# Local attention: the query projection of a tile moved ahead of the output projection and the scores on TensorE

## The chip, the core and the metric

The kernel runs on one core of a Trainium2 chip. The time is the device time of the launch in microseconds (us), as the median of the runs; the profile is one execution of the same program. Five queues work side by side and meet only at semaphores: TensorE (PE; its weight loads are listed as PEld), VectorE (DVE), ScalarE (ACT), GpSimd (POOL) and SyncE (SP), which issues transfers.

## The reference, cut to what matters

Four blocks stand in a row: cross attention, a feed-forward block that is a two-layer local transformer, cross attention again, and a mixture of experts. The change touches the local attention inside the second block, which runs once for each of its two layers (16 sequences of 256 tokens, 8 heads of 64, windows of 64 tokens):

```python
def _layer(x, wqkv, qs, ksc, wo, ...):
    h = shift_token(x)
    q, k, v = jnp.split(h @ wqkv, 3, axis=-1)     # then split into heads
    q = l2norm(q) * qs
    k = l2norm(k) * ksc
    q, k = rotary_xpos(q, k)
    o = local_attention(q, k, v)                  # own and previous window
    x = x + o @ wo
    ...                                           # feed-forward part
```

The order in which the tiles' projections are computed has no effect on the values.

## The kernel before

The 16 x 256 tokens are 32 tiles of 128 tokens (T = 32). Class Local holds local attention as a software pipeline: in step s each engine works on several tiles of different age, and its program is written out by hand, step after step. Nothing is scheduled by a tool; every engine runs its own list in order and waits where a semaphore tells it to. Local runs for l = 0 and l = 1, one tile in each step.

In a step s, TensorE's list (method tensor) is:

- the values of tile s-4 into the bank ps_b (project_h, three 128x512 matmuls at L947 to L949);
- the output projection of tile s-7 into ps_a (L990);
- the masks and scores of tile s-4 into ps_s (L1004 and L963);
- the queries of tile s-1 into the first half of ps_qk (project_h again);
- the transposes of rotated queries and keys of tile s-3 (L1032) and of the input of tile s (L1043);
- attention weights times values of tile s-6 (L1057), the transposes of the weights of tile s-5 (L1068);
- the keys of tile s-1 into the second half of ps_qk.

VectorE's list in the same step (method vector) is: reciprocal of the softmax sums of tile s-5 (L1174), addition of the output projection of tile s-7 to the residual (L1178, "the y addition" below), the sums of squares of tile s-2 (L1184), the row maxima of the scores of tile s-4 (L1191) and their scaling (L1195), the copy of transposed queries of tile s-3 (L1202), the two products of the keys' rotation of tile s-2 (L1156, L1158), the copy of the attention output of tile s-6 (L1215), the low part of the transposed input of tile s (L1221), and last the two products of the queries' rotation of tile s-1 (L1156, L1158 again).

ps_qk has one copy. So the query projection of tile s-1 may overwrite its first half only when ScalarE has squared the queries of tile s-2 out of it and VectorE has rotated them, which is the last thing on VectorE's list in step s-1. Two lines of the projection say so, with k the number of the tile counted over both layers:

```python
after(pe, self.s_sq, 2 * (k - 1) + 1)
after(pe, self.s_r, 4 * (k - 1) + 2)
```

GpSimd adds the two products of a rotation (L1260 for queries, L1272 for keys), multiplies the exponentials by the reciprocal (L1266) and scales the keys (L1279). ScalarE squares queries and keys (L1103, L1142), takes the eight exponentials of a tile (L1135) and copies transposed results. The neighbouring stages overlap the first and the last steps of Local.

Of the kernel before, what the change touches and what calls it, by code (L numbers as in the profile page):

```python
# [19 lines left out]
T = B * S // P  # L20
# [6 lines left out]
INNER = LH * LD  # L27
# [74 lines left out]
def after(eng, sem, count):  # L102

    if count > 0:
        eng.wait_ge(sem, count)
# [775 lines left out]
class Local(Phase):  # L881
# [83 lines left out]
    def tensor(self, pe, l, s):  # L965
        g = self.g
        ps_qk, ps_t, ps_a, ps_b, ps_s = self.banks[l]
# [6 lines left out]
        n = s - 4  # L974
        if 0 <= n < T:
            k = T * l + n
            after(pe, self.s_vc, k)
            after(pe, self.s_oc, k - 2)
            if n == 0:
                self.take(pe, l, "b")  # L980
            self.project_h(pe, ps_b[:, :], n, 1024).then_inc(self.s_v, 1)
        n = s - 7
        if 0 <= n < T:
            k = T * l + n
# [8 lines left out]
        n = s - 4  # L993
        if 0 <= n < T:
            k, u, b = T * l + n, n % 2, n // 2
# [12 lines left out]
                    for x in range(2):  # L1008
                        m = self.scores(pe, ps_s, pair, e, x, u, b)
            m.then_inc(self.s_s, 1)  # L1010
        n = s - 1
        if 0 <= n < T:
            k = T * l + n
            pe.wait_ge(self.s_hc, k + 1)
            pe.wait_ge(self.s_hr, k + 1)
            after(pe, self.s_sq, 2 * (k - 1) + 1)
            after(pe, self.s_r, 4 * (k - 1) + 2)
            if n == 0:
                self.take(pe, l, "qk")
            self.project_h(pe, ps_qk[:, 0:INNER], n, 0).then_inc(self.s_qk, 1)  # L1020
        n = s - 3
        if 0 <= n < T:
            k = T * l + n
# [10 lines left out]
        n = s  # L1034
        if 0 <= n < T:
            k = T * l + n
# [7 lines left out]
        n = s - 6  # L1044
        if 0 <= n < T:
            k, u, b = T * l + n, n % 2, n // 2
# [14 lines left out]
        n = s - 5  # L1061
        if 0 <= n < T:
            k = T * l + n
# [6 lines left out]
        n = s - 1  # L1070
        if 0 <= n < T:
            k = T * l + n
# [750 lines left out]
```

## Time and profile before

| | |
|---|---|
| median of 3 runs | 1166.66 us (1161.32 to 1167.23) |
| the profiled execution's own time | 1164.99 us |
| its span, first to last instruction | 1162.5 us |
| PE busy | 1074.8 us (92%) |
| DVE busy | 967.7 us (83%) |
| ACT busy | 932.1 us (80%) |
| POOL busy | 762.9 us (66%) |

Local attention occupies about 165 to 420 us and 500 to 770 us of the span. In the steady part of either layer a step takes 7.62 us. Busy shares say little by themselves here: what counts is, for each engine's list, which of its waits ends last.

### The profile page before, as it was taken

Reading aid. Unit: us, or ns where it says so; the run is one execution under the profiler, and the core shown is the slowest. Engines: PE = TensorE matmul, PEld = TensorE weight load, DVE = VectorE, ACT = ScalarE, POOL = GpSimd, SP = SyncE. Lnnn points to the kernel's source line nnn. Section 1 sums busy time; section 2 is a strip of 40 time slices with the busy share of each in tenths; the row PEclk is TensorE's granted clock in tenths of the full one; section 3 lists DMA queues with packets and bytes.
Section 4 is the critical chain, followed back from the end, with each engine's and each line's share of the span. In section 5 each row is a group of like instructions: output and inputs, shape, how many; then the busy total and the mean of one; then the engine's idle time right before and its main releaser. Section 6 shows DMA issues by size and latency. Waiting matters only on the chain.

```text
span 1162.5 us, 33084 instructions
## 1 busy us (share of the span) xinstructions
PE 1074.8 (92%) x11244; PEld 911.1 (78%) x11244; DVE 967.7 (83%) x2205; ACT 932.1 (80%) x2588; POOL 762.9 (66%) x1182
## 2 busy tenths in 40 slices
PE   6899977999999989979999999989899997999996
PEld 3777755888887869967888888789777775899996
DVE  4799967998899856768999999758889997599988
ACT  4898966999999977649999999967578886867662
POOL 5799956767777766647766777646779993344431
PEclk9999998999999999989999999999989998999998
DMA  6100000211111101101112311100000000000000
GB/s 200 25 2 1 2 15 17 56 30 29 27 25 31 25 18 29 24 15 28 24 30 47 84 27 25 25 16 18 3 2 2 3 1 2 6 15 12 16 14 16
DMA packets 53157, 28.65 MB, mean 25 GB/s; under 512 B 36949, under 2 KB 47233, under 8 KB 52994
## 3 DMA queue, kind: packets, MB, share of 16 engines
q1 hardware_dynamic: 50370, 25.83, 9.1%
q8 instruction: 93, 1.52, 0.6%
q10 hardware_dynamic: 2624, 0.72, 0.3%
q14 instruction: 70, 0.57, 0.2%
HBM read 9.77 MB, written 2.10 MB: 10 GB/s over the span
## 4 chain that ended last, share of the span: by engine, by line
PE 63%; DVE 14%; ACT 10%; issue 8%; POOL 4%; DMA 0%; ACTq 0%; DVEq 0%; POOLq 0%
PE m_ps_y L1609 7%; PE a_ps_b L1057 5%; PE a_ps_s L963 5%; PE a_ps_t L1032 5%; PE a_ps_t L1068 5%; PE a_ps_a L990 4%; PE a_ps_qk L947 4%; DVE x_e L708 3%; PE f_ps_y L1376 3%; PE a_ps_qk L948 2%; PE a_ps_qk L949 2%; PE a_ps_s L1004 2%; PE m_ps_h L1596 2%; PE m_ps_h L1597 2%; PE m_ps_h L1598 2%
## 5 line engine op out<-in xcount | busy, mean ns | idle before, releaser
L1135 ACT ACTIVATE a_e<-a_ps_s,a_stat 128x128 f32<-128x128 f32 x512 | 226.8, 476 | 5.1 <-DVE a_stat L1195 5.1
L1272 POOL TENSOR_TENSOR a_rot<-a_rot 128x512 f32<-128x512 f32 x64 | 82.8, 1293 | 138.7 <-DVE a_rot L1158 138.7
L1266 POOL TENSOR_TENSOR a_e<-a_e,a_stat 128x1024 f32<-128x1024 f32 x64 | 121.4, 1898 | 2.7 <-DVE a_stat L1174 2.7
L1135 ACT ACTIVATION_READ_ACCUMULATOR a_e<-a_ps_s,a_stat 128x1 f32 x512 | 114.7, 224 | 0.0
L1260 POOL TENSOR_TENSOR a_rot<-a_rot 128x512 f32<-128x512 f32 x64 | 81.7, 1277 | 15.4 <-DVE a_rot L1158 15.4
L757 DVE TENSOR_REDUCE x_stat<-x_ps_s 128x16 f32<-128x1024 f32 x64 | 77.1, 1205 | 12.0 <-PE x_ps_s L563 12.0
L1158 DVE TENSOR_TENSOR a_rot<-a_ps_qk,a_rtab 128x512 f32<-128x512 f32 x128 | 87.1, 680 | 0.0
L1156 DVE TENSOR_TENSOR a_rot<-a_ps_qk,a_rtab 128x512 f32<-128x512 f32 x128 | 87.0, 680 | 0.0
L1191 DVE TENSOR_REDUCE a_stat<-a_ps_s 128x8 f32<-128x1024 f32 x64 | 77.8, 1216 | 7.2 <-PE a_ps_s L963 7.2
L1184 DVE TENSOR_REDUCE a_stat<-a_sq 128x16 f32<-128x1024 f32 x64 | 77.9, 1218 | 3.0 <-ACT a_sq L1142 1.5
L708 DVE TENSOR_TENSOR x_e<-x_ps_s,x_stat 128x512 f32<-128x512 f32 (+1 forms) x96 | 79.3, 852 | 1.0 <-PE x_ps_t L606 1.0
L1068 PE MATMUL a_ps_t<-c,a_e 128*128 128x128 f32 x512 | 69.6, 279 | 7.7 <-POOL a_e L1266 2.6
L947 PE MATMUL a_ps_qk<-a_wqh,a_hT 128*128 128x512 f32 x128 | 63.4, 495 | 13.9 <-DVE a_rot L1158 13.5
L1057 PE MATMUL a_ps_b<-a_eT,a_vt 128*64 128x64 f32 x1536 | 68.5, 224 | 4.0 <-ACT a_eT L1148 4.0
L990 PEld LDWEIGHTS a_ps_a<-lwo,a_oT 128*128 128x128 f32 x512 | 67.4, 193 | 5.9 <-DVE a_oT L1215 0.7
L1148 ACT ACTIVATE a_eT<-a_ps_t 128x1024 f32<-128x1024 f32 x64 | 68.5, 1070 | 4.3 <-PE a_ps_t L1068 4.3
L606 PE MATMUL x_ps_t<-c,x_e 128*128 128x128 f32 x512 | 70.8, 282 | 0.7 <-ACT x_e L669 0.7
L1279 POOL TENSOR_TENSOR a_rot<-a_rot,a_stat 128x512 f32<-128x512 f32 x64 | 66.9, 1045 | 5.0
L853 POOL TENSOR_TENSOR x_khm<-kTm,c 65x512 fp32r<-65x512 f32 x64 | 65.7, 1046 | 6.3 <-ACT kTm L408 3.3
L669 ACT ACTIVATE x_e<-x_e 128x1024 f32<-128x1024 f32 x64 | 67.5, 1054 | 2.6 <-DVE x_e L708 2.6
L963 PE MATMUL a_ps_s<-a_kTr,a_qT 64*64 64x128 f32 x2048 | 69.4, 273 | 0.0
L990 PE MATMUL a_ps_a<-lwo,a_oT 128*128 128x128 f32 x512 | 68.4, 277 | 0.5 <-DVE a_oT L1215 0.5
(221 smaller groups left out, 3684.5 us busy)
## 6 DMA issues: line engine op xcount, KB each, us to landing
a_vx<-a_vt SPq DMA_DIRECT2D x64, 128.0 KB, 2.3
a_h<-y SPq DMA_DIRECT2D x64, 32.0 KB
out_dram<-x SPq DMA_DIRECT2D x32, 64.0 KB, 1.5
a_h<-y SPq DMA_DIRECT2D x64, 31.8 KB
f_h<-y SPq DMA_DIRECT2D x32, 63.5 KB
wqkv<-in_L_ffn_wqkv_dram SPq DMA_DIRECT2D x2, 768.0 KB, 4.9
w<-in_L_ffn_w_dram SPq DMA_DIRECT2D x2, 768.0 KB, 5.5
x<-in_x_dram SPq DMA_DIRECT2D x1, 768.0 KB, 5.2
```

Source lines behind the costliest of these rows:

```text
L708: v.tensor_tensor(self.e[n % 2][:, at].rearrange("p (h k) -> p h k", k=SC), ps_s[:, at].rearrange("p (h k) -> p h k", k=SC), self.stat[n % ...
L947: pe.matmul(dst, h[:, :], self.wqh[:, lo:lo + 512], start=True, stop=False)
L963: return pe.matmul(dst, self.qT[u][rows, P * pair + WIN * x:P * pair + WIN * x + WIN], ky, start=False, stop=(pair == LP - 1))
L990: m = pe.matmul(ps_a[:, 0:D], self.oT[n % 2][:, P * pair:P * pair + P], g.lwo[:, D * pair:D * pair + D], start=(pair == 0), stop=(pair == ...
L1057: m = pe.matmul(ps_b[LD * e:LD * e + LD, P * pair + WIN * x:P * pair + WIN * x + WIN], vv[:, P * pair + LD * e:P * pair + LD * e + LD], se ...
L1068: m = pe.transpose(ps_t[:, P * i:P * i + P], self.e[n % 2][:, P * i:P * i + P], g.ident)
L1135: act.activation(self.e[n % 2][:, P * i:P * i + P], ps_s[:, P * i:P * i + P], ACT.Exp, bias=stat[:, 24 + i:25 + i], scale=stat[:, root:roo ...
L1156: v.tensor_tensor(out1, qk, cos_.unsqueeze(1).broadcast_to([P, LH, LD]), ALU.mult).then_inc(self.s_r, 1)
L1158: v.tensor_tensor(out2.rearrange("p h (o d) -> p h o d", o=2), swapped, sin_.rearrange("p (o d) -> p o d", o=2).unsqueeze(1).broadcast_to( ...
L1260: p.tensor_tensor(r, r, self.rot2[:, 0:INNER], ALU.add).then_inc(self.s_nq, 1)
L1266: p.tensor_tensor(e3, e3, self.stat[n % UNROLL][:, 16:24].unsqueeze(2).broadcast_to([P, 8, P]), ALU.mult)\
L1272: p.tensor_tensor(r, r, self.rot2[:, INNER:], ALU.add).then_inc(self.s_n, 1)
```

## The change

Only the place of one block in TensorE's list changes: the query projection of tile s-1 stands directly behind the values of tile s-4, ahead of the output projection of tile s-7 and the scores of tile s-4. Its waits go with it unaltered. The lists of the other engines are the same.

```diff
             self.project_h(pe, ps_b[:, :], n, 1024).then_inc(self.s_v, 1)
+        n = s - 1
+        if 0 <= n < T:
+            k = T * l + n
+            pe.wait_ge(self.s_hc, k + 1)
+            pe.wait_ge(self.s_hr, k + 1)
+            after(pe, self.s_sq, 2 * (k - 1) + 1)
+            after(pe, self.s_r, 4 * (k - 1) + 2)
+            if n == 0:
+                self.take(pe, l, "qk")
+            self.project_h(pe, ps_qk[:, 0:INNER], n, 0).then_inc(self.s_qk, 1)
         n = s - 7
...
             m.then_inc(self.s_s, 1)
-        n = s - 1
-        if 0 <= n < T:
-            k = T * l + n
-            pe.wait_ge(self.s_hc, k + 1)
-            pe.wait_ge(self.s_hr, k + 1)
-            after(pe, self.s_sq, 2 * (k - 1) + 1)
-            after(pe, self.s_r, 4 * (k - 1) + 2)
-            if n == 0:
-                self.take(pe, l, "qk")
-            self.project_h(pe, ps_qk[:, 0:INNER], n, 0).then_inc(self.s_qk, 1)
         n = s - 3
```

TensorE in a steady step of layer 0, before: ps_b is the bank of the values, ps_a that of the output projection, ps_s that of the scores, ps_qk that of queries and keys; what stands in brackets are the semaphores waited for, among them a_r (rotation products by VectorE), a_sq (squares by ScalarE), a_y and a_yc (output projection done and added), a_e (exponentials) and a_oc (attention output copied).

```order
L949 MATMUL a_ps_b0<-a_wqh,a_hTr0 128x512
L990 MATMUL a_ps_a0<-lwo,a_oT1 128x128 [waits a_hc,a_hr,a_yc,a_oc]
L990 MATMUL a_ps_a0<-lwo,a_oT1 128x128 x3
L1004 MATMUL a_ps_s0<-c16 64x512 [waits a_e,a_kc,a_qc]
L1004 MATMUL a_ps_s0<-c16 64x512 x3
L963 MATMUL a_ps_s0<-a_kTr0,a_qT0 64x128 x16
L947 MATMUL a_ps_qk0<-a_wqh,a_hT3 128x512 [waits a_sq,a_r,a_hr,a_hc]
L948 MATMUL a_ps_qk0<-a_wqr,a_hT3 128x512
L949 MATMUL a_ps_qk0<-a_wqh,a_hTr3 128x512
L1032 MATMUL a_ps_t0<-c32,a_rot1 128x128 [waits a_qc,a_ec,a_kc,a_nq,a_n]
```

The same place of TensorE's list in the changed kernel, where the lines behind the inserted block have numbers 10 higher (L1000 and L1014 for L990 and L1004):

```order
L949 MATMUL a_ps_b0<-a_wqh,a_hTr0 128x512
L947 MATMUL a_ps_qk0<-a_wqh,a_hT3 128x512 [waits a_sq,a_r,a_hr,a_hc]
L948 MATMUL a_ps_qk0<-a_wqr,a_hT3 128x512
L949 MATMUL a_ps_qk0<-a_wqh,a_hTr3 128x512
L1000 MATMUL a_ps_a0<-lwo,a_oT1 128x128 [waits a_hc,a_hr,a_yc,a_oc]
L1000 MATMUL a_ps_a0<-lwo,a_oT1 128x128 x3
L1014 MATMUL a_ps_s0<-c16 64x512 [waits a_e,a_kc,a_qc]
L1014 MATMUL a_ps_s0<-c16 64x512 x3
L963 MATMUL a_ps_s0<-a_kTr0,a_qT0 64x128 x16
L1032 MATMUL a_ps_t0<-c32,a_rot1 128x128 [waits a_qc,a_ec,a_kc,a_nq,a_n]
```

The three matmuls with the wait on a_r now stand between the values and the output projection, and the transposes follow the scores directly.

VectorE around the same place, in the changed kernel and in the one before alike: the end of step s-1 and the beginning of step s.

```order
L1156 TENSOR_TENSOR a_rot1<-a_ps_qk0,a_rtab 128x512 [waits a_nq,a_t,a_sq]
L1158 TENSOR_TENSOR a_rot2<-a_ps_qk0,a_rtab 128x512
L1174 RECIPROCAL a_stat2<-a_stat2 128x8 [waits a_e]
L1178 TENSOR_TENSOR y<-a_ps_a0,y 128x128 [waits a_y]
L1184 TENSOR_REDUCE a_stat1<-a_sq 128x16 [waits a_rt,a_sq]
L1191 TENSOR_REDUCE a_stat3<-a_ps_s0 128x8 [waits a_en,a_s]
L1195 TENSOR_TENSOR a_stat3<-a_stat3 128x8 [waits a_rt,a_mx]
L1202 COPY a_qT0<-a_ps_t0 128x512 [waits a_s,a_t]
```

Nothing moved here: the first two rows are the queries' rotation that a_r counts, the fourth is the y addition that waits for the output projection.

## Rows read from the trace of the kernel before

**Rows 1.** The page, chain that ended last: shares of the span by engine.
```profile
PE 63%; DVE 14%; ACT 10%; issue 8%; POOL 4%; DMA 0%; ACTq 0%; DVEq 0%; POOLq 0%
```

**Rows 2.** Timeline, VectorE, steady step: start us, us, engine, line, operation [idle before].
```profile
307.12 0.68 DVE L1158 TENSOR_TENSOR a_rot<-a_ps_qk,a_rtab 128x512 f32<-128x512 f32 x1
308.35 0.20 DVE L1174 RECIPROCAL a_stat<-a_stat 128x8 f32<-128x8 f32 x1 [0.55 <-ACT a_e L1135]
308.51 0.29 DVE L1178 TENSOR_TENSOR y<-a_ps_a,y 128x128 f32<-128x128 f32 x1
308.84 1.22 DVE L1184 TENSOR_REDUCE a_stat<-a_sq 128x16 f32<-128x1024 f32 x1
309.98 1.22 DVE L1191 TENSOR_REDUCE a_stat<-a_ps_s 128x8 f32<-128x1024 f32 x1
311.23 0.21 DVE L1195 TENSOR_TENSOR a_stat<-a_stat 128x8 f32<-128x8 f32 x1
311.55 0.69 DVE L1202 COPY a_qT<-a_ps_t 128x512 f32<-128x512 f32 x1
...
312.75 0.68 DVE L1158 TENSOR_TENSOR a_rot<-a_ps_qk,a_rtab 128x512 f32<-128x512 f32 x1
...
314.75 0.68 DVE L1158 TENSOR_TENSOR a_rot<-a_ps_qk,a_rtab 128x512 f32<-128x512 f32 x1
315.97 0.20 DVE L1174 RECIPROCAL a_stat<-a_stat 128x8 f32<-128x8 f32 x1 [0.55 <-ACT a_e L1135]
```

**Rows 3.** Timeline, TensorE, the same step.
```profile
307.20 0.39 PE L949 MATMUL a_ps_b<-a_wqh,a_hTr 128*128 128x512 f32 x1
307.42 1.05 PE L990 MATMUL a_ps_a<-lwo,a_oT 128*128 128x128 f32 x8
...
308.68 1.07 PE L963 MATMUL a_ps_s<-a_kTr,a_qT 64*64 64x128 f32 x32
309.68 0.50 PE L947 MATMUL a_ps_qk<-a_wqh,a_hT 128*128 128x512 f32 x1
```

**Rows 4.** Timeline, step 3 of layer 0: TensorE held by VectorE.
```profile
181.71 0.68 DVE L1158 TENSOR_TENSOR a_rot<-a_ps_qk,a_rtab 128x512 f32<-128x512 f32 x1
...
182.54 0.47 PE L947 MATMUL a_ps_qk<-a_wqh,a_hT 128*128 128x512 f32 x1 [1.96 <-DVE a_rot L1158]
...
183.31 0.40 PE L947 MATMUL a_ps_b<-a_wqh,a_hT 128*128 128x512 f32 x1
```

**Rows 5.** Timeline, VectorE, two steps with more GpSimd work beside them.
```profile
363.10 0.29 DVE L1178 TENSOR_TENSOR y<-a_ps_a,y 128x128 f32<-128x128 f32 x1 [0.59 <-PE a_ps_a L990]
363.31 1.21 DVE L1184 TENSOR_REDUCE a_stat<-a_sq 128x16 f32<-128x1024 f32 x1
364.43 1.22 DVE L1191 TENSOR_REDUCE a_stat<-a_ps_s 128x8 f32<-128x1024 f32 x1
365.68 1.21 DVE L1195 TENSOR_TENSOR a_stat<-a_stat 128x8 f32<-128x8 f32 x1
...
374.21 0.17 DVE L1195 TENSOR_TENSOR a_stat<-a_stat 128x8 f32<-128x8 f32 x1
374.36 0.69 DVE L1202 COPY a_qT<-a_ps_t 128x512 f32<-128x512 f32 x1
```

**Rows 6.** Timeline, GpSimd, the steady step and the step of 363 us.
```profile
313.51 1.29 POOL L1272 TENSOR_TENSOR a_rot<-a_rot 128x512 f32<-128x512 f32 x1 [2.10 <-DVE a_rot L1158]
...
317.12 1.89 POOL L1266 TENSOR_TENSOR a_e<-a_e,a_stat 128x1024 f32<-128x1024 f32 x1
...
362.84 0.93 POOL L1495 TENSOR_TENSOR kT<-mw,kT 128x341 fp32r<-128x341 f32 x1
...
364.98 1.90 POOL L1266 TENSOR_TENSOR a_e<-a_e,a_stat 128x1024 f32<-128x1024 f32 x1
```

**Rows 7.** Timeline, ScalarE: the keys' squares after the last exponential.
```profile
315.79 0.64 ACT L1142 ACTIVATE a_sq<-a_ps_qk 128x512 f32<-128x512 f32 x1
```

**Rows 8.** Timeline, VectorE: last query rotation product of steps 6 and 32, both layers.
```profile
208.09 0.68 DVE L1158 TENSOR_TENSOR a_rot<-a_ps_qk,a_rtab 128x512 f32<-128x512 f32 x1
...
407.84 0.68 DVE L1158 TENSOR_TENSOR a_rot<-a_ps_qk,a_rtab 128x512 f32<-128x512 f32 x1
...
539.05 0.68 DVE L1158 TENSOR_TENSOR a_rot<-a_ps_qk,a_rtab 128x512 f32<-128x512 f32 x1
...
738.37 0.68 DVE L1158 TENSOR_TENSOR a_rot<-a_ps_qk,a_rtab 128x512 f32<-128x512 f32 x1
```

## The prediction

> **What bounds the kernel now.** I read the chain that ended last first: TensorE carries 63% of it [rows 1], so a change that only filled a hole in TensorE's list would pay. Then I read one steady step of 7.62 us on each engine, because a share does not say which wait ends last. TensorE runs almost without a hole: values, output projection from 307.42, scores, queries from 309.68 [rows 3]. VectorE is nearly as full. It ends the queries' rotation at 307.12 + 0.68 = 307.80, idles 0.55 us, runs the reciprocal, and starts the y addition at 308.51 [rows 2]. The output projection ends at 307.42 + 1.05 = 308.47 [rows 3]. So the y addition already starts only 0.04 us after TensorE gives it its input, and where the output projection came later the profile names it as the releaser of an idle 0.59 us [rows 5]. That is the first thing to see: **VectorE has no slack against the output projection**. The second is when the moved block becomes ready. It may overwrite ps_qk only once the queries' rotation of the tile before is done, at 307.80 in this step. Today it starts at 309.68, 1.9 us later, and never notices. At its new place TensorE reaches it right behind the last matmul of the values at 307.20 [rows 3], and finds it not ready.
>
> **The change part by part.** No instruction is added or removed and no other engine's list changes; TensorE's 3 query matmuls move, in each of 32 steps of each layer, past the output projection (tile s-7) and the scores (tile s-4).
>
> The wait that appears. The values' last matmul starts at 307.20 and the next could start 0.22 us later, at 307.42 [rows 3]. The release of the rotation reaches TensorE's matmul 0.15 us after VectorE's product ends: 181.71 + 0.68 = 182.39, matmul at 182.54, with the hole before it put down to this product [rows 4]. So TensorE holds from 307.42 to 307.95. Queued behind it are the output projection and the scores, and VectorE's y addition waits for the former. Behind the y addition stands all the rest of VectorE's step, which ends in the very rotation that releases the next query projection. That closes a ring through two engines, and its length is the new step.
>
> The ring, TensorE's part: 0.15 release; 0.77 from the first query matmul to the first matmul behind the three (182.54 to 183.31, [rows 4]); 1.05 output projection [rows 3]; 0.04 to the y addition. Sum 2.01 us, from the end of the queries' rotation to the start of the y addition. Today that stretch is 308.51 - 307.80 = 0.71 us.
>
> The ring, VectorE's part: today from the y addition to the end of the queries' rotation it is 314.75 + 0.68 - 308.51 = 6.92 us [rows 2]. Two small holes in it close. The sums of squares start 0.33 us after the y addition, since ScalarE's squares end at 315.79 + 0.64 = 316.43 of the next step, 0.46 us after the reciprocal's start [rows 2, 7]; when those squares are early the gap is 363.31 - 363.10 = 0.21 us [rows 5]. That gives back 0.12. The copy of transposed queries starts 0.32 us after the scaling L1195, waiting for TensorE's transposes; the nearest row of a short gap is 374.36 - 374.21 = 0.15 us [rows 5], and the transposes come sooner, as no query projection stands ahead of them. That gives back 0.17. So 6.92 - 0.12 - 0.17 = 6.63 us. From the other side these two terms are bounded by zero, if neither hole closes.
>
> **The new step is 2.01 + 6.63 = 8.64 us**, between 8.6 (the copy following a little closer) and 8.93 (no hole closes).
>
> What else could end last in a step of that length:
> - The scores. They end today 308.68 + 1.07 - 308.47 = 1.28 us after the output projection [rows 3], that is 1.24 after the y addition's start; the maxima are wanted 0.21 + 1.12 = 1.33 after it [rows 5]. On time by 0.1 us.
> - ScalarE. From the end of the sums of squares (308.84 + 1.22 = 310.06) through ScalarE's small steps and eight exponentials to the next reciprocal (315.97) it takes 5.91 us [rows 2]. In the new step that is 0.21 + 1.21 + 5.91 = 7.33 us after the y addition, and the next y addition comes at 8.64. 1.3 us to spare, so ScalarE and its 0.55 us hold on VectorE drop out.
> - TensorE. The key projection waits for the keys' rotation, done at 312.75 + 0.68 = 313.43, 2.00 us ahead of the queries' [rows 2]; 2.00 - 2 x 0.77, for keys and values, leaves some 0.5 us of holding before the queries. TensorE turns from the engine without holes into one that waits in each step.
> - GpSimd. Its multiplication L1266 starts 317.12 - 315.43 = 1.69 us after the queries' rotation ends and lasts 1.89 [rows 2, 6], so it is over at 3.58; VectorE's L1195 comes at 2.01 + 0.21 + 1.12 + 1.25 = 4.59. They no longer meet.
>
> How many steps. The ring needs both a query projection (s up to 32) and an output projection (s from 7), so it turns 26 times in a layer, from the queries' rotation of step 6 to that of step 32. Today those stretches take 407.84 - 208.09 = 199.75 us and 738.37 - 539.05 = 199.32 us [rows 8], 399.1 in all; that holds a few steps of 8.2 to 8.3 us, where L1195 met the longer GpSimd queue. New: 52 x 8.64 = 449.3 us. **The difference is +50 us.** Steps 1 to 3 keep their order in effect. In steps 4 to 6 the maxima wait for the query projection and the scores: 0.15 + 0.77 + 1.28 + 0.04 = 2.24 us after the rotation's end, then 6.63 - 1.33 = 5.30 more, 7.54 in all, no longer than today's step; I put those 6 steps at nothing, between -1 and +3 us. After step 32 no query projection is left and the old order returns: nothing, within 2 us.
>
> The profiled execution took 1164.99 us: 1165.0 + 50.2 = 1215.2 us. It lies 1.7 us under the median and inside the three runs' range, so I leave the sum as it is: **1215**.
>
> **The rivals.**
>
> Faster (the move fills holes and nothing is held): if the rotation were done before TensorE arrives, the transposes would follow the scores at once, ScalarE's exponentials would start earlier, and VectorE's two small holes of 0.12 and 0.17 us would close without a new one. At most 52 x 0.29 = 15 us would come back: 1150 us. The point from which it decides is a rotation that ends before 307.42 - 0.15 = 307.27. It ends at 307.80, in every steady step, and slowing nothing else makes it earlier. Chance 0.03. That the change does nothing is out: the lists show the three matmuls moved and each engine runs its list in order.
>
> Only TensorE's hold is paid (slower, by less): 307.95 - 307.42 = 0.53 us a step, and VectorE swallows the later y addition: 52 x 0.53 = 28 us, 1193 us. It needs slack of VectorE behind the y addition. Apart from the two small holes, counted above, there is none, and its 0.55 us hole lies ahead of the y addition, where it is used up: the y addition moves by 1.3. Chance 0.06.
>
> A collision with GpSimd in each step (slower, by more). VectorE's L1195 works on 128x8 numbers and takes 0.17 us alone, but 1.21 us at 365.68, when GpSimd's L1266 was under way from 364.98 to 366.88; it ended with it [rows 5, 6]. If the two met again in each step at that price, 52 x 1.04 = 54 us would come on top: 1269 us. It would take a GpSimd queue 1.0 us later against VectorE than worked out above (3.58 against 4.59). In the few steps with L1495 (0.93 us, [rows 6]) the margin shrinks to 0.1, so a few tenths may show there. Chance 0.04. The Trainium skill, page "SBUF — State Buffer", section "Who interferes with whom", says that a VectorE instruction with two SBUF inputs contends with a GpSimd instruction that reads SBUF, and that the one issued second is held until the first finishes; by that rule L1195 belongs to the risky kind and the PSUM readers around it do not, and the trace agrees with its 1.21 us.
>
> **How the numbers follow.** Forecast 0.87 (1215, its own range 1205 to 1227: step 8.5 to 8.75, edges within 4 us), only the hold 0.06, collision 0.04, faster 0.03. The upper bound of 8.93 a step would give 1165 + 52 x 8.93 - 399.1 = 1230. The range of 8 in 10 is 1204 to 1228. About 0.5% is what a measurement of this kernel can tell from no change. Faster by more than that: 0.03; within: 0.02, if the hold proves half as long and is swallowed; slower: 0.95.
>
> **What the profile after would show.** Steady steps of 8.6 us in place of 7.62. TensorE's query matmul with an idle stretch before it put down to VectorE's rotation, dozens of times. VectorE's y addition idle about 1.2 to 1.5 us before it, put down to the output projection, 52 times, and no more idle before the reciprocal. L1195 at 0.17 us. ScalarE with more than 1 us of idle in each step, before the activation that waits for the sums of squares. Everything outside local attention shifted, not longer. I would be wrong if the y addition did not wait for TensorE, if L1195 took above 1 us throughout, or if the steps stayed at 7.6.

## The result and the profile after

| | before | after |
|---|---|---|
| median | 1166.08 us | 1209.03 us |
| ratio | | 1.0375 (95% interval 1.0347 to 1.0402) |
| span of the profiled execution | 1162.5 us | 1206.2 us |
| steady step of local attention | 7.62 us | 8.54 us |

Of the four executions of the changed kernel one took 1488.71 us, at a granted clock of 0.65 where the others had 0.98; the ratio leaves it out, and the median of the other three is 1208.98 us. The change makes the kernel slower by 43 us; 1215 us with a range of 1204 to 1228 had been forecast.

VectorE in a steady step of layer 0 of the changed kernel, to be held against [rows 2] (start us, us, engine, line, operation, idle time before it and its releaser):

```profile
303.39 0.68 DVE L1158 TENSOR_TENSOR a_rot<-a_ps_qk,a_rtab 128x512 f32<-128x512 f32 x1
304.28 0.20 DVE L1174 RECIPROCAL a_stat<-a_stat 128x8 f32<-128x8 f32 x1 [0.21 <-ACT a_e L1135]
306.08 0.29 DVE L1178 TENSOR_TENSOR y<-a_ps_a,y 128x128 f32<-128x128 f32 x1 [1.59 <-PE a_ps_a L1000]
306.29 1.21 DVE L1184 TENSOR_REDUCE a_stat<-a_sq 128x16 f32<-128x1024 f32 x1
307.41 1.21 DVE L1191 TENSOR_REDUCE a_stat<-a_ps_s 128x8 f32<-128x1024 f32 x1
308.66 0.17 DVE L1195 TENSOR_TENSOR a_stat<-a_stat 128x8 f32<-128x8 f32 x1
308.74 0.69 DVE L1202 COPY a_qT<-a_ps_t 128x512 f32<-128x512 f32 x1
...
311.93 0.68 DVE L1158 TENSOR_TENSOR a_rot<-a_ps_qk,a_rtab 128x512 f32<-128x512 f32 x1
```

TensorE in the same step, to be held against [rows 3]:

```profile
303.46 0.39 PE L949 MATMUL a_ps_b<-a_wqh,a_hTr 128*128 128x512 f32 x1
304.21 0.47 PE L947 MATMUL a_ps_qk<-a_wqh,a_hT 128*128 128x512 f32 x1 [0.36 <-DVE a_rot L1158]
...
304.99 1.05 PE L1000 MATMUL a_ps_a<-lwo,a_oT 128*128 128x128 f32 x8
305.97 0.41 PE L1014 MATMUL a_ps_s<-c 64*64 64x512 bf16 x4
306.21 1.04 PE L963 MATMUL a_ps_s<-a_kTr,a_qT 64*64 64x128 f32 x32
307.18 1.09 PE L1032 MATMUL a_ps_t<-c,a_rot 128*128 128x128 f32 x8
```

Read them together as a ring. VectorE's rotation of the queries ends at 303.39 + 0.68 = 304.07. 0.14 us later TensorE starts the query projection that waited for it. The output projection follows at 304.99 and ends at 306.04; the y addition (L1178) starts at 306.08, after 1.59 us in which VectorE had nothing to do. VectorE then works without a hole until the next rotation ends at 311.93 + 0.68 = 312.61. That is 2.01 us through TensorE and 6.53 us on VectorE, 8.54 us in all. Of the waits over the whole kernel these bear on the ring (us in total, times, longest; the third counts query and key projections together):

```profile
DVE y L1178 <- PE a_ps_a L1000: 88.6, 60, 2.1
...
ACT a_stat L1097 <- DVE a_stat L1184: 76.3, 57, 2.2
...
PE a_ps_qk L947 <- DVE a_rot L1158: 40.8, 115, 2.6
...
DVE a_stat L1174 <- ACT a_e L1135: 21.8, 61, 2.7
```

The second row is ScalarE waiting for the sums of squares, which VectorE computes behind the y addition. It is late through the ring and no cause of it: ScalarE's last exponential holds VectorE only ahead of the reciprocal, and VectorE waits there for the output projection in any case.

A warning on the chain of waits. The page of the changed kernel gives GpSimd 16% of it, where before it had 4% [rows 1]:

```profile
PE 32%; DVE 26%; issue 17%; POOL 16%; ACT 9%; DMA 0%; DVEq 0%; ACTq 0%; POOLq 0%
```

The chain in order of time shows why, first as it runs through most of layer 0 (start us, us, what):

```profile
303.53 1.04 POOL a_rot L1279
304.57 1.25 POOL a_rot L1260
305.82 1.85 POOL a_e L1266
307.67 2.99 issue
```

and then in layer 1:

```profile
561.65 0.61 DVE a_rot L1158
562.40 0.47 PE a_ps_qk L947
...
563.33 0.90 PE a_ps_a L1000 x8
...
564.46 1.08 DVE a_stat L1184
...
565.59 1.22 DVE a_stat L1191
```

Both layers take the same 8.54 us a step. In layer 0 the chain ran along GpSimd's own list and bridged 2.99 us of each step by "issue", which is no work of any engine; a chain that needs so much of it has lost the way. GpSimd's next instruction there, L1272, does wait for something, VectorE's rotation products of the keys:

```profile
310.70 1.30 POOL L1272 TENSOR_TENSOR a_rot<-a_rot 128x512 f32<-128x512 f32 x1 [3.03 <-DVE a_rot L1158]
```

In layer 1 the chain is the ring.

### The profile page after: what moved, and what is told of

Same layout as the page of the kernel before. It is cut to its first block, busy times and chain, and to the rows that moved or that the text cites. A ratio compares the mean times of both kernels' runs of the same rounds, so it can differ in the third digit from the quotient of the medians.

```text
span 1206.2 us, 33084 instructions
## 1 busy us (share of the span) xinstructions
PE 1088.7 (90%) x11244; PEld 902.0 (75%) x11244; DVE 953.8 (79%) x2205; ACT 926.0 (77%) x2588; POOL 763.3 (63%) x1182
## 4 chain that ended last, share of the span: by engine, by line
PE 32%; DVE 26%; issue 17%; POOL 16%; ACT 9%; DMA 0%; DVEq 0%; ACTq 0%; POOLq 0%
PE m_ps_y L1609 6%; DVE a_stat L1191 4%; POOL a_e L1266 4%; DVE a_rot L1158 4%; DVE x_e L708 3%; DVE a_stat L1184 3%; PE a_ps_a L1000 3%; POOL a_rot L1272 3%; POOL a_rot L1260 3%; PE f_ps_y L1376 2%; DVE a_rot L1156 2%; POOL a_rot L1279 2%; PE m_ps_h L1596 2%; PE m_ps_h L1598 2%; PE m_ps_h L1597 2%
## 5 line engine op out<-in xcount | busy, mean ns | idle before, releaser
L1272 POOL TENSOR_TENSOR a_rot<-a_rot 128x512 f32<-128x512 f32 x64 | 82.7, 1292 | 183.9 <-DVE a_rot L1158 183.9
L1178 DVE TENSOR_TENSOR y<-a_ps_a,y 128x128 f32<-128x128 f32 x64 | 18.5, 289 | 88.6 <-PE a_ps_a L1000 88.6
L947 PEld LDWEIGHTS a_ps_qk<-a_wqh,a_hT 128*128 128x128 f32 x128 | 24.8, 194 | 78.0 <-issue 73.6
L1184 DVE TENSOR_REDUCE a_stat<-a_sq 128x16 f32<-128x1024 f32 x64 | 77.4, 1209 | 1.7 <-ACT a_sq L1142 1.5
L1097 ACT ACTIVATE a_stat<-a_stat,small 128x16 f32<-128x16 f32 x64 | 19.6, 307 | 76.3 <-DVE a_stat L1184 76.3
L1032 PE MATMUL a_ps_t<-c,a_rot 128*128 128x128 f32 x512 | 71.5, 284 | 0.0
L1000 PEld LDWEIGHTS a_ps_a<-lwo,a_oT 128*128 128x128 f32 x512 | 66.8, 192 | 5.8 <-DVE a_oT L1215 0.7
```

Source lines behind the costliest of these rows:

```text
L947: pe.matmul(dst, h[:, :], self.wqh[:, lo:lo + 512], start=True, stop=False)
L1000: m = pe.matmul(ps_a[:, 0:D], self.oT[n % 2][:, P * pair:P * pair + P], g.lwo[:, D * pair:D * pair + D], start=(pair == 0), stop=(pair == ...
L1184: v.reduce_sum(self.stat[n % UNROLL][:, 32:48], self.sq[:, :].rearrange("p (h d) -> p h d", d=LD), axis=AX_X)\
L1272: p.tensor_tensor(r, r, self.rot2[:, INNER:], ALU.add).then_inc(self.s_n, 1)
```

## The experiments

Three explanations were held against each other: the ring; a cost of TensorE's new order as such, whatever VectorE does; and a cost of the hold alone, or of the y addition alone.

Each ratio below is taken against the kernel before, run again beside the experiment. Its medians were 1165.59 us beside the half move, the short rotation in the changed kernel, the y addition and the early rotation in the changed kernel; 1162.79 us beside the short and the early rotation in the kernel before, the first steps and the query projection directly ahead of the keys; 1166.02 us beside the low part last, the one layer and the last kernel. So two medians from different occasions can differ by some 3 us without a cause in the kernel.

**Half of the move.** The query projection behind the output projection, ahead of the scores.

```diff
 (output projection)
+        (query projection of tile s-1)
 (scores)
-        (query projection of tile s-1)
```

> Half of the move: the query projection stands behind the output projection and ahead of the scores. Theory: TensorE reaches it after the rotation has ended, so no hold; the y addition comes as early as before, but the scores are 0.70 us later and VectorE's maxima wait for them: 0.14 + 0.77 + 0.70 + 0.98 + 0.70 + 1.28 + 0.04 = 4.6 from the keys' rotation to the maxima and 3.21 back, 7.82 us a step, 52 x 0.15 = 8 us more than the kernel before (after a mean step of 7.67): 1174 us. Rival A (the order as such costs 1 us): about 1209 us. Rival B (only what is held costs): nothing is held, so 1166 us.

Measured 1178.06 us, ratio 1.0101 (1.0076 to 1.0126), 7.88 us a step. VectorE:

```profile
306.41 0.20 DVE L1174 RECIPROCAL a_stat<-a_stat 128x8 f32<-128x8 f32 x1 [0.20 <-ACT a_e L1135]
306.93 0.29 DVE L1178 TENSOR_TENSOR y<-a_ps_a,y 128x128 f32<-128x128 f32 x1 [0.32 <-PE a_ps_a L990]
307.14 1.21 DVE L1184 TENSOR_REDUCE a_stat<-a_sq 128x16 f32<-128x1024 f32 x1
308.88 1.22 DVE L1191 TENSOR_REDUCE a_stat<-a_ps_s 128x8 f32<-128x1024 f32 x1 [0.53 <-PE a_ps_s L963]
```

The wait for the scores takes the place of the wait for the output projection, as the ring theory has it. Neither the order as such (1209) nor "only what is held costs" (1166) gives this number; the forecast of 1174 was 4 us low, 3 of them from 52 steps that are 0.06 us longer than reckoned. Nothing holds the query projection in this kernel, and a step still costs 0.26 us more than before.

**The rotation shortened**, in the changed kernel and in the one before. The second product of the queries' rotation covers 1 of 8 heads; for the other seven it is left out, so these two kernels do not compute the reference's values.

```diff
-        swapped = qk.rearrange(...)[:, :, ::-1, :]
+        m = LH if i else 1
+        swapped = qk.rearrange(...)[:, 0:m, ::-1, :]
```

> The changed kernel with the second product of the queries' rotation taken over 1 of 8 heads (the rest of that half is left out of the sum; the scratch is cleared once). It shortens VectorE's last instruction of a step from 0.60 to about 0.15 us. Theory: this instruction lies on the ring, so each of 52 steps gives back 0.45 to 0.5 us: 8.06 us a step, 24 us less than the changed kernel, 1185 us. Rival A (order as such): nothing, 1209 us.

Measured 1186.53 us, ratio 1.0177 (1.0153 to 1.0202), 8.08 us a step.

```profile
305.06 0.21 DVE L1159 TENSOR_TENSOR a_rot<-a_ps_qk,a_rtab 128x64 f32<-128x64 f32 x1
```

> The same shortening in the kernel before (second product of the queries' rotation over 1 of 8 heads, the rest left out). Theory: there the rotation ends 0.55 us before VectorE's next wait and 1.9 us before the queries are projected, so it is on no ring: 7.62 us a step as before, 1166 us within 3 us. If it gained 20 us here too, the shortening would prove nothing about the ring.

Measured 1161.33 us, ratio 0.9985 (0.9969 to 1.0002), 7.62 us a step, not a hundredth less than before. The time saved turns up as idle time of VectorE, which waits 1.02 us for ScalarE where it waited 0.55 [rows 2]:

```profile
305.73 0.20 DVE L1176 RECIPROCAL a_stat<-a_stat 128x8 f32<-128x8 f32 x1 [1.02 <-ACT a_e L1135]
```

So the same 0.47 us of VectorE's work is worth 0.46 us a step in the changed kernel and nothing in the old one. This pair is the strongest evidence for the ring: the changed kernel put the rotation on it. A hold without a ring would shrink with the rotation too; the size tells them apart. The changed kernel loses 0.92 us a step where the hold is 0.53, and with the short rotation, which would leave 0.06 of that hold, it still loses 0.46.

**The y addition behind the sums of squares**, in the changed kernel.

```diff
+        (sums of squares, L1184)
         n = s - 7
         if 0 <= n < T:
             v.wait_ge(self.s_y, T * l + n + 1)
...
-        (sums of squares, L1184)
```

> The changed kernel with VectorE's y addition moved behind the sums of squares, so that 1.2 us of VectorE's work fill its wait. Theory: the y addition is the first but not the only thing that waits; the scores end 1.28 us behind the output projection and the maxima wait for them, so the ring shortens only from 8.54 to 0.14 + 0.77 + 0.98 + 1.28 + 0.04 + 5.20 = 8.42 us: 6 us less, 1203 us. Rival C (the y addition alone carries the loss): the step loses 1.2 us, 1150 to 1166 us.

Measured 1206.21 us, ratio 1.0348 (1.0309 to 1.0387), 8.47 us a step. By the medians alone that cannot be told from the changed kernel; the step of the profile is 0.07 us shorter, where 0.12 had been expected.

```profile
304.55 1.22 DVE L1180 TENSOR_REDUCE a_stat<-a_sq 128x16 f32<-128x1024 f32 x1 [0.29 <-ACT a_sq L1142]
305.87 0.29 DVE L1185 TENSOR_TENSOR y<-a_ps_a,y 128x128 f32<-128x128 f32 x1
307.12 1.22 DVE L1191 TENSOR_REDUCE a_stat<-a_ps_s 128x8 f32<-128x1024 f32 x1 [0.96 <-PE a_ps_s L963]
```

The wait of the y addition is gone completely and the time is nearly all still there. The 88.6 us in the list of waits are what the profile books to the first late input; the second, the scores, stands right behind it. What costs is the place of the query projection ahead of both.

**The rotation earlier.** In both kernels VectorE rotates the queries ahead of the copy of the attention output (a_oT) and of the low part of the input (a_hTr).

```diff
+        (rotation of the queries of tile s-1)
         n = s - 6
...          v.tensor_copy(self.oT[n % 2][:, :], ps_b[:, :])
...
-        (rotation of the queries of tile s-1)
```

> The changed kernel with VectorE's rotation of the queries moved ahead of the copy of the attention output and of the low part of the input; TensorE's list is that of the changed kernel. Theory (a ring from the end of the queries' rotation through query projection, output projection and y addition back to the rotation): the rotation ends 0.8 us sooner, so the queries are no longer held; what is left is the ring from the keys' rotation through keys, values, queries, output projection to the y addition, 0.14 + 0.77 + 0.70 + 0.70 + 1.05 + 0.04 = 3.4, plus 4.54 on VectorE from the y addition to the end of the keys' rotation: 7.95 us a step in place of 8.54, 52 x 0.59 = 31 us less than the changed kernel, about 1178 us. Rival A (TensorE's new order costs its 1 us by itself, through changes of tile shape or weight loads): VectorE's order is of no account, still 1209 us.

Measured 1231.29 us, ratio 1.0570 (1.0540 to 1.0601), 9.03 us a step: slower by 22 us where 31 us faster had been expected.

> The kernel before with the queries' rotation ahead of the copy of the attention output and of the low part of the input on VectorE. Control to the same edit of the changed kernel. Theory: no gain, since nothing of the kernel before waits for this rotation: 1166 us, within 5 us (the queries' squares may hold the rotation by some tenths).

Measured 1217.34 us, ratio 1.0462 (1.0443 to 1.0480), 8.67 us a step: also a clear miss. TensorE there:

```profile
314.46 0.47 PE L947 MATMUL a_ps_b<-a_wqh,a_hT 128*128 128x512 f32 x1 [0.86 <-DVE a_oT L1222]
```

Both had the same cause, one that I had not looked at. The value projection writes the bank ps_b, so it waits until the attention output of the step before has been copied out of it:

```python
after(pe, self.s_oc, k - 2)
...
self.project_h(pe, ps_b[:, :], n, 1024).then_inc(self.s_v, 1)
```

The edit moved that copy back by the rotation's 1.2 us. Reckoned afterwards from its own trace, the ring of the first kernel reads: y addition to the end of that copy 6.34 us, 0.14 + 0.77 for the values, 0.70 queries, 1.05 output projection, 0.04, together 9.04 us against 9.03 measured. In the kernel before the queries are not on it: 6.68 from the y addition to the end of the copy, 0.15, 0.77, 1.05 and 0.03, together 8.68 us against 8.67. The experiment failed as a test of the rotation's release; that the same sums come out around another release speaks for the way of reckoning, though nobody forecast them.

**The low part last**, in the changed kernel: the rotation only ahead of the low part.

```diff
+        (rotation of the queries of tile s-1)
         n = s
...          v.tensor_tensor(self.hTr[r][:, :], ps_a[:, 0:P], self.hT[r][:, :], ALU.subtract)
-        (rotation of the queries of tile s-1)
```

> The changed kernel with VectorE's last two pieces of a step exchanged: the rotation of the queries ahead of the low part of the input (L1221), which is now last; the rotation ends 0.2 us sooner. The query projection waits for both. Theory with two releases: the low part of the tile that is projected now ends where the rotation ended (6.54 us after the y addition in place of 6.53), so the step stays at 8.54 us and the time at 1207 us. Were the rotation the only release, the step would fall to 8.34 and the time to 1197 us.

Measured 1203.04 us, ratio 1.0317 (1.0298 to 1.0336), 8.50 us a step.

```profile
309.73 0.28 DVE L1228 TENSOR_TENSOR a_hTr<-a_ps_a,a_hT 128x128 fp32r<-128x128 f32 x1
...
310.11 0.47 PE L947 MATMUL a_ps_qk<-a_wqh,a_hT 128*128 128x512 f32 x1 [0.31 <-DVE a_hTr L1228]
```

The profile now names the low part as the releaser. The rotation alone would have allowed 8.34; 0.04 us a step came, not 0.20, and it came from the release: TensorE starts 0.10 us after the low part ends (310.01 to 310.11), where it starts 0.14 after the rotation. Over 52 steps that is 2 us; the profiled executions differ by 2.3 us, the medians by 6, and the rest of those 6 is not explained. Whatever stands last on VectorE's list holds the query projection, since it needs both.

**One layer only, and the first steps only.** A condition picks the early or the old place: `l == 0`, and in another kernel `s <= 6`.

> The move in layer 0 alone; layer 1 keeps the order of the kernel before. Theory: the loss is a sum over steps, 26 x 8.54 = 222.0 us against 199.75 before, 22 us more than the kernel before: about 1186 us, half of the whole change's. If one layer carried the loss it would be 0 or 43.

Measured 1187.32 us, ratio 1.0171 (1.0144 to 1.0198); 8.54 us a step in layer 0 and 7.63 in layer 1. Half the steps, half the loss.

> The early place of the query projection only in steps up to 6 of both layers, where no output projection stands behind it. Theory: these steps lack the ring through the y addition; the forecast put them at nothing, -1 to +3 us: 1166 us, within 3. Rival B (each held query projection costs): 6 steps x 0.5 us, the same size, so this run only bounds the edges. Rival A (order as such costs 1 us a step): 10 us more, 1176 us.

Measured 1163.84 us, ratio 1.0008 (0.9993 to 1.0023). Where no output projection stands behind the query projection, its early place costs nothing that can be measured (by the interval, at most 3 us).

**The opposite move.** The query projection to the end of the step, in the kernel before, ahead of the key projection; ScalarE squares the queries between its exponentials.

```diff
-        (query projection of tile s-1, behind the scores)
...
+        (query projection of tile s-1)
         (key projection of tile s-1)
```

> The opposite move, in the kernel before: the query projection goes to the end of the step, directly ahead of the key projection, and ScalarE squares the queries between the sixth and seventh exponential. Theory: nothing is held, the queries leave the stretch between scores and transposes, which stood on ScalarE's way to the exponentials, and the three products queries, keys and values follow one another on TensorE; the first matmul behind the scores takes 0.43 us there and 0.23 behind another product. TensorE's own work of about 7.4 us sets the step: 52 to 64 x 0.2 = 10 to 13 us less, 1155 us. Rival D (the ring from the keys' rotation to the y addition sets 7.6 us whatever the queries do): 1166 us.

Measured 1173.01 us, ratio 1.0083 (1.0067 to 1.0100), 7.83 us a step, slower where 1155 us had been expected.

```profile
309.84 0.69 DVE L1157 TENSOR_TENSOR a_rot<-a_ps_qk,a_rtab 128x512 f32<-128x512 f32 x1 [0.71 <-ACT a_sq L1137]
...
313.89 0.47 DVE L1196 TENSOR_TENSOR a_stat<-a_stat 128x8 f32<-128x8 f32 x1
```

The queries come so late that VectorE waits 0.71 us for their squares, and its small product L1196 runs into GpSimd's multiplication. That multiplication starts at 312.45 us, and L1196 ends 0.02 us behind it:

```profile
312.45 1.89 POOL L1267 TENSOR_TENSOR a_e<-a_e,a_stat 128x1024 f32<-128x1024 f32 x1
```

TensorE stood still for 0.39 us ahead of the transposes of the weights, so there was room one place earlier. The next kernel puts the query projection there, and ScalarE's squares behind the third exponential:

> The kernel before with the query projection between the products of weights and values and the transposes of the weights of the next tile, and ScalarE's squares of the queries behind the third exponential. The variant ahead of the key projection took 7.83 us a step, since VectorE's rotation waited 0.71 us for those squares, while TensorE idled 0.39 us ahead of the transposes. Here the projection fills that idle time and the squares are 0.9 us sooner. Theory: the rotation is not held, and the step is set by TensorE's own work or by VectorE's 4.54 + 0.3 and 2.63 us around the ring of the keys: 7.4 to 7.5 us a step, 52 x 0.2 = 10 us less than the kernel before, 1155 us. If the rotation is still held or VectorE's L1195 meets GpSimd: 7.6 to 7.8, 1163 to 1172 us.

Measured 1160.10 us, ratio 0.9950 (0.9935 to 0.9965), 7.60 us a step: faster than both kernels, by half of what was expected against the kernel before; none of its six executions is as slow as any of the eleven of the kernel before that were run beside it. VectorE:

```profile
303.72 0.68 DVE L1157 TENSOR_TENSOR a_rot<-a_ps_qk,a_rtab 128x512 f32<-128x512 f32 x1
304.32 0.68 DVE L1159 TENSOR_TENSOR a_rot<-a_ps_qk,a_rtab 128x512 f32<-128x512 f32 x1
305.77 0.20 DVE L1175 RECIPROCAL a_stat<-a_stat 128x8 f32<-128x8 f32 x1 [0.77 <-ACT a_e L1130]
```

ScalarE, and TensorE's transposes behind the scores:

```profile
306.09 1.06 ACT L1149 ACTIVATE a_eT<-a_ps_t 128x1024 f32<-128x1024 f32 x1
...
306.22 1.04 PE L963 MATMUL a_ps_s<-a_kTr,a_qT 64*64 64x128 f32 x32
307.35 1.06 PE L1022 MATMUL a_ps_t<-c,a_rot 128*128 128x128 f32 x8
```

The rotation is no longer held. Now VectorE waits 0.77 us for the exponentials, and the transposes start 307.35 - 306.22 = 1.13 us after the scores where in the changed kernel it is 0.97. They write the bank that ScalarE's copy at 306.09 reads until 307.15, so that copy is the likely holder; no run tested it. The steps of [rows 8] give only 1.4 us in both layers together (199.17 and 198.47 us against 199.75 and 199.32). Of the 6.1 us by which the profiled executions differ, 2.6 lie ahead of step 6 of layer 0 and 3.3 between step 32 of layer 0 and step 6 of layer 1. The granted clock of TensorE was higher in part of these steps: 1.00 from 180 to 190 us against 0.83 in the kernel before, and 0.97 from 508 to 520 us against 0.87 from 512 to 525. Whether the new place or the clock shortened those steps is not shown. Both kernels of this opposite move also shift ScalarE's squares, so they do not tell what the query projection's place does by itself.

## Why the prediction was right, and where its sizes were off

The mechanism was right: the hold, the ring behind it, and 26 turns of it in each layer. Of its numbers:

- The hold: 0.53 us reckoned; measured from 303.46 + 0.22 to 304.21, 0.53 us.
- TensorE's part of the ring: 2.01 reckoned, 2.01 measured. The release and the three matmuls came from rows in which TensorE had been held by VectorE before [rows 4], the output projection from the steady step [rows 3].
- VectorE's part: 6.63 reckoned, 6.53 measured. The mis-sized term is the gap from the scaling L1195 to the copy of the queries. I had taken 0.15 us from 374.21 and 374.36 [rows 5], where the copy still waited for TensorE: the transposes at 373.29 end at 374.32. Free of that it is 308.74 - 308.66 = 0.08 us. The remaining 0.03 is spread over several distances, 0.02 of it between the two reductions (1.12 for 1.14). 52 x 0.10 = 5.2 us.
- The number of steps: the two stretches took 222.2 and 221.9 us against 199.75 and 199.32 [rows 8], together 45.0 us more, where 50.2 had been forecast. The spans differ by 43.7, so everything outside these stretches is 1.4 us shorter: 1.3 longer ahead of the first, 1.2 shorter between the two, 1.5 shorter behind the second. That is no credit of the first and last steps, which the forecast put at nothing: behind the last y addition, where local attention is over, 391.6 us stand against 394.0, at a granted clock of 0.97 against 0.96; up to there the first and last steps come out 1.0 us longer, inside what was allowed for them. The run with one layer bears out the count of steps, the run with the first steps alone that they cost nothing.
- What else could end last: scores and ScalarE stayed in time, GpSimd too. Its multiplication starts at 314.32 and lasts 1.90 us, so it ends 1.0 us ahead of L1195 of that step. L1195 took 0.17 us in each of the 52 steps; the collisions before [rows 5, 6] are gone from them. Seven longer ones, of 0.34 to 1.64 us, are left ahead of step 6 and behind step 32. One step of layer 0 took 8.80 us, since its sums of squares came 0.24 us late, for no reason that the profile names. By the Trainium skill, page "SBUF — State Buffer", section "Who interferes with whom", a VectorE instruction with two SBUF inputs is held when a GpSimd instruction that reads SBUF was issued before it. In the 52 steps that had nothing to act on; the trace of the opposite move agrees with it, where L1196 took 0.47 us and ended with GpSimd's multiplication.
- The signs: idle before the y addition 1.59 us where 1.2 to 1.5 had been named, in 60 steps, as the last steps of a layer count too. The forecast that no idle time would be left before the reciprocal was wrong: 0.21 us remained, without effect. The prediction's own numbers say so, since they put the reciprocal's input 7.33 us behind the y addition and the end of VectorE's list at 6.63; it had compared the 7.33 with the next y addition only. Measured are 6.75 and 6.53.

The rivals fell one by one. Only the hold (1193 us): the loss is 0.92 us a step against 0.53 of hold, and VectorE had no slack. Faster: the rotation was not done in time in any steady step. Collision: none in the 52 steps. What the forecast had overlooked did no harm to it but spoilt two experiments: the value projection's own wait for a bank of PSUM.

## What to carry to other kernels

Before a block is moved forward in an in-order queue, look up when its last input is ready, and compare that with the time at which the queue reaches the new place; then ask who waits for what stands behind it. If that engine's list leads back to the awaited input, the stall is no one-off but the sum around a ring, paid in each step, and it can be worked out from start-to-start distances to a tenth of a microsecond. Of a ring, list every wait that could close it: filling one hole (the y addition) gave 0.07 us a step, moving the rotation forward on VectorE's list gave 0.04 or made it worse, because a second wait stood within a few tenths. Only less work on the ring (the short rotation) came back in full.

## What the runs showed of the hardware

TensorE's matmul started 0.14 to 0.15 us after the profiled end of a rotation product or copy of 128x512 by VectorE that it had waited for, and 0.10 us after the low part of 128x128. The other way, the y addition started 0.03 to 0.04 us after the output projection's profiled end, and the row maxima 0.08 us after that of the scores. And a VectorE instruction on 128x8 numbers took 0.17 us alone and 1.21 us beside GpSimd's multiplication, by nothing but the moment at which it came [rows 5, 6]; there it ended 0.01 us behind the multiplication, and in the opposite move 0.02 us behind it.
